# Deformable-convolution stage: waiting for the landing of the tile ahead in front of every second tile only

## The reference

```
offset  = conv2d(x, offset_w)                       # 18 maps: (dy, dx) for each of 9 taps
sy, sx  = base_y + dy, base_x + dx                  # where each tap of each pixel reads
y0, x0  = floor(sy), floor(sx);  ly, lx = sy - y0, sx - x0
p  = corner(y0,   x0,   (1-ly)*(1-lx)) + corner(y0,   x0+1, (1-ly)*lx)
p += corner(y0+1, x0,   ly*(1-lx))     + corner(y0+1, x0+1, ly*lx)   # gathered by index
y  = einsum('bckhw,ock->bohw', p, wk)               # [32, 64, 56, 56]
out = x + y * sigmoid(mean(y) + std(y))             # mean and std of each image and channel
```

## Time and profile before

| | |
|---|---|
| median of three runs | 15,070.81 us (15,065.17 to 15,072.31) |
| the profiled execution | 15,021.82 us |
| its span on the core | 15,020.2 us |
| mean granted clock of TensorE | 0.733 of full speed |
| busy: TensorE / weight load | 8857.2 us (59%) / 6070.3 us (40%) |
| busy: GpSimd / VectorE / ScalarE | 7518.3 us (50%) / 6520.5 us (43%) / 3085.6 us (21%) |
| first and last gather start | 3864.2 us and 14,983.5 us |

### The profile page before, as it was taken

One profiled execution on the slowest core, in us unless ns is written; L12 is line 12 of the kernel. 1 busy time (PEld: TensorE's weight loads), 2 busy tenths in 40 slices (PEclk: granted clock), 3 DMA queues, 4 the chain that ended last, 5 costly groups with the idle time before them and its releaser, 6 DMA issues.

```text
span 15020.2 us, 156851 instructions
## 1 busy us (share of the span) xinstructions
PE 8857.2 (59%) x51639; PEld 6070.3 (40%) x51639; DVE 6520.5 (43%) x13120; ACT 3085.6 (21%) x5214; POOL 7518.3 (50%) x7657
## 2 busy tenths in 40 slices
PE   6897888888554544545454545454454545454543
PEld 2333444448443433333343434343343434343433
DVE  5655556553334444343434343434434343434333
ACT  3433444432111111111111111111111111111111
POOL 0011222212466666666666666666666666666665
PEclk9998999989666666767676766666666657676766
DMA  3322111126333333333333333333333333333332
GB/s 95 84 82 66 52 60 56 56 99 189 96 91 109 91 108 99 101 99 101 106 96 103 98 109 91 109 91 109 99 102 102 98 103 96 104 98 109 91 94 83
DMA packets 503924, 1436.05 MB, mean 96 GB/s; under 512 B 128980, under 2 KB 234196, under 8 KB 474576
## 3 DMA queue, kind: packets, MB, share of 16 engines
q0 software_dynamic: 353344, 970.88, 22.2%
q1 hardware_dynamic: 150032, 458.00, 10.1%
HBM read 1175.46 MB, written 252.90 MB: 95 GB/s over the span
## 4 chain that ended last, share of the span: by engine, by line
POOL 29%; issue 19%; DMA 13%; DVE 8%; PE 6%; another core or an unknown queue 0%; DVEq 0%; POOLq 0%; ACT 0%; ACTq 0%; SPq 0%
POOL e_g L1786 29%; DMA e_g<-table_dram,e_index_slots 12%; DVE e_g L2050 2%; PE e_ps L1903 2%; DVE e_g L2052 2%; PE e_ps L1918 2%; PE e_ps L1930 2%; PE e_ps L1939 1%; DMA e_tmp<-x3s_dram 1%; DVE e_x3t L1963 1%; DVE e_index_slots L2024 1%; DVE e_x3t L1967 0%; DVE e_w_next L2008 0%; DVE e_st L1971 0%
## 5 line engine op out<-in xcount | busy, mean ns | idle before, releaser
L1786 POOL DMA_INDIRECT e_g<-table_dram,e_index_slots x7056 | 6823.6, 967 | 4426.0 <-issue 1893.4
L1930 PE MATMUL e_ps<-k_ident,e_g 128*128 128x128 f32 x7056 | 1719.1, 398 | 4897.7 <-DVE e_g L2052 4840.2
L1930 PEld LDWEIGHTS e_ps<-k_ident,e_g 128*128 128x128 f32 x7056 | 1153.8, 197 | 5455.4 <-DVE e_g L2052 5209.6
L1939 PE MATMUL e_ps<-e_corners,e_w_def 128*64 128x128 f32 x14112 | 2667.5, 369 | 268.6 <-issue 148.9
L2024 DVE COPY e_index_slots<-e_index_now 128x9 uint32<-128x9 uint32 (+1 forms) x784 | 137.9, 177 | 5866.8 <-DMA e_g<-table_dram,e_index_slots 4314.5
L1939 PEld LDWEIGHTS e_ps<-e_corners,e_w_def 128*64 128x64 f32 x14112 | 2430.1, 197 | 463.7 <-issue 319.0
L1855 ACT ACTIVATE e_corners<-e_ps 128x512 f32<-128x512 f32 (+1 forms) x2352 | 1064.7, 489 | 4603.2 <-PE e_ps L1930 3895.9
L2049 DVE TENSOR_TENSOR e_ps<-e_g,e_ps 128x512 f32<-128x512 f32 (+1 forms) x2352 | 1324.5, 563 | 115.6 <-DMA e_g<-table_dram,e_index_slots 61.1
L2052 DVE TENSOR_TENSOR e_g<-e_g,e_ps 128x512 f32<-128x512 f32 (+1 forms) x2352 | 1301.5, 553 | 81.3
L2050 DVE TENSOR_TENSOR e_g<-e_g,e_ps 128x512 f32<-128x512 f32 (+1 forms) x2352 | 1284.8, 546 | 0.0
L1860 ACT ACTIVATE e_big<-e_ps 64x128 f32<-64x128 f32 (+1 forms) x784 | 211.8, 270 | 3518.7 <-remote 2210.0
(11 more groups left out here) (438 smaller groups left out, 8075.1 us busy)
## 6 DMA issues: line engine op xcount, KB each, us to landing
e_g<-table_dram,e_index_slots POOLq DMA_INDIRECT x7056
table_dram<-e_rt SPq DMA_DIRECT2D x32, 1624.0 KB
a_xt<-x_in SPq DMA_DIRECT2D x16, 1568.0 KB
v_dram<-a_vout SPq DMA_DIRECT2D x32, 784.0 KB, 8.5
b_xt<-v_dram SPq DMA_DIRECT2D x16, 1568.0 KB
v_dram<-b_vout SPq DMA_DIRECT2D x32, 784.0 KB, 7.5
c_v2t<-v_dram SPq DMA_DIRECT2D x16, 1568.0 KB
c_xt<-x_in SPq DMA_DIRECT2D x16, 1568.0 KB, 6.6
```

Source lines behind the costliest of these rows:

```text
L1786: pool.indirect_dma_start(out=g[:, slot, tap * CORNERS:(tap + 1) * CORNERS], out_offset=None, in_=table, in_offset=bass.IndirectOffsetOnAx ...
L1930: mm = pe.transpose(ps[:, TURN[tap // 4], (tap % 4) * P:(tap % 4 + 1) * P], g[:, slot, tap * CORNERS:tap * CORNERS + 2 * C], k.ident[:, :])
L1939: mm = pe.matmul(ps[0:C, OUT, 0:P], w_d[:, tap, :], corners[:, tap, :], start=(tap == 0), stop=(tap == TAPS - 1))
```

## The change

GpSimd's wait for the landing of the tile ahead is kept in front of slots 2, 4 and 6 of the prologue and in front of slots 0, 2, 4 and 6 of every later round. In front of slots 1, 3 and 5 it is left out. The waits for the freed slot and for the indices stay everywhere, as do the order and number of the gathers. VectorE still waits for each slot's own landing.

```
                 for slot in range(SLOTS):
                     pool.wait_ge(index_ready, slot + 1)
-                    if slot:
+                    if slot and slot % 2 == 0:
                         pool.wait_ge(gathered[slot - 1], 16 * TAPS)
                     gather(slot)
                 with pool.Fori(1, PAIRS * GROUPS) as r:
                     for slot in range(SLOTS):
 
                         pool.wait_ge(bank_done, (r - 1) * (3 * SLOTS) + (3 * slot + 3))
-                        pool.wait_ge(gathered[(slot - 1) % SLOTS], r * (16 * TAPS) + (16 * TAPS if slot else 0))
+                        if slot % 2 == 0:
+                            pool.wait_ge(gathered[(slot - 1) % SLOTS], r * (16 * TAPS) + (16 * TAPS if slot else 0))
                         pause(pool, index_ready, r * SLOTS + (slot + 1), passed)
                         gather(slot)
```

## The result

The forecast was 14,110 us. The changed kernel takes **15,669 us** (median of four runs, 15,639 to 15,713) against 15,068 us of the kernel before: a ratio of 1.040, interval 1.037 to 1.043. It is 4% slower, and loaded a second time it took 15,843 us (1.053, 1.051 to 1.055). Both lie above the range and on the wrong side. The profiled execution took 15,712.6 us; its span is 690.7 us longer than that of before (15,710.9 against 15,020.2).

The account below looks back on a forecast made before the run. The prediction took GpSimd's chain of gather descriptors and landing waits to bound the deform stage. Dropped waits (810 us) plus stretched gaps (150 us) gave 960 us off 15,070.8, so 14,110 us, range 14,005 to 14,265.

Parts of the forecast that it names:

- What bounds the kernel now: Deform stage: GpSimd's chain of writing gather descriptors and waiting for landings, 13.6 us a tile, 10,700 us over 784 tiles.
- the false releaser at line 2024: VectorE's index copy, named by the page for 548 gaps; claimed to end together with the gap, both awaiting the same landing.
- the sequencer's cover: GpSimd's sequencer runs ahead; six queued gathers, some 7 us, hide the remaining waits, leaving 0.30 us at dropped waits.
- the first rival: Half the gap stays: uncovered sequencer work leaves 1.21 us at each dropped wait, 14,420 us; chance 0.08.
- The two terms of the sum: 336 dropped waits at 2.41 us give 810 us; stretched gaps beside bulk transfers give 150 us of 255.
- Nothing downstream is near its limit: Slots are freed early enough; per 697 us pair VectorE is busy 280 us and TensorE 350 us.
- The 50 us of the tightest refill: Smallest distance from VectorE's end of a tile to GpSimd's refill of its slot: 50.2 us of 777 refills, median 78.
- The waits that stay: In front of slots 0, 2, 4 and 6 GpSimd still waits 2.71 us, landing lag stays 1.8 us, cost 0.
- The sum: 810 + 150 = 960 us saved, taking 15,070.8 to 14,110 us, 6.4% faster.
- the gathers wait for something else: Rival: VectorE's index copy or the freed slot truly releases the gathers, so nothing changes, 15,070 us; chance 0.02.
- The slower rival: With up to 18 gathers under way the descriptor writer waits for room, each second-tile gather stretched 0.50 us, 15,780 us; chance 0.03.
- The signs named in the forecast: Expected profile: dropped gaps 0.30 us, gathers 946 ns, pair period near 637 us; freed-slot waits becoming real would mean wrong.

Follow-up runs that it names:

- e11: Changed kernel plus a waited-for one-column memset inside every tile, placed so no run of gathers exceeds six: 14,548 us, ratio 0.967.
- e10: Changed kernel plus a waited-for one-column memset after the fifth gather of every tile: 14,851 and, loaded again, 14,860 us, ratio 0.988 and 0.987.
- e7: Kernel before plus a waited-for one-column memset after the fifth gather of every tile: 15,777 us, ratio 1.051.
- e1: Changed kernel, its remaining landing waits kept, each gather also waiting for the landing of the third one before: 15,140 us, ratio 1.005.
- e2: Changed kernel without landing waits in front of any slot, each gather waiting for the landing of the third one before: 15,897 us, ratio 1.055.
- e6: Changed kernel with gathers of 512 bytes per pixel instead of 1 KB, part of the computation left out: 15,943 us, ratio 1.061.
- e3: Changed kernel plus a waited-for one-column memset in front of slots 1, 3 and 5: 14,672, 15,612 and 15,550 us in three loads.
- e5: Changed kernel without landing waits, a waited-for one-column memset in front of each slot but the first instead: 16,015 us, ratio 1.067.
- e4: Changed kernel with GpSimd's landing waits taken out for every slot, nothing in their place: 16,242 us, ratio 1.078.

## Why the prediction was wrong, step by step

*What bounds the kernel now*: right about GpSimd's chain and about the false releaser at line 2024. The dropped waits left 0.30, 0.43 and 0.38 us, as forecast, with the sequencer's cover as argued; the first rival (1.21 us) is refuted. The two terms of the sum, 810 + 150 = 960 us, measured 961 us together at the dropped waits.

*"Nothing downstream is near its limit"* is **the step that failed**. The 50 us of the tightest refill were read as slack of a chain whose own times stay. They did not stay: the delay from TensorE to ScalarE tripled with the length of GpSimd's runs, on the one pair of engines that every tile passes in order. In sum the 784 delays grew from 1418 to 4264 us, 25 us more in each round of seven tiles. The transposes' signals came late on top. That these delays and the shorter period that was wanted together used up the 50 us is argued from these sums; that the distance fell to 1.5 us and slot 0 waited in 90 of 111 rounds is counted. One entry of the page of before pointed there and was not followed: "remote" released 2210 us of ScalarE's idle time at line 1860, the largest entry there. Busy shares, which I used, do not show a late signal. And a range whose only uncertain terms were the landing lag and the excess had no term for what the runs of 18 do to others.

*The waits that stay* were put at a cost of 0, and here the whole loss stands: 1498 us in front of slot 0 and 178 us in front of slots 2, 4 and 6. The latter are 3.9, 3.5 and 3.2 us in the mean against 3.41, 2.84 and 2.72 before; the medians of slots 2 and 4 went to 4.2 and 4.0 us, and in the main the profile names "remote" as their releaser, not a landing.

*The sum* was right where the signals do come in time. For e11 it says 14,110 + 784 breaks: 498 us more of gaps within tiles were counted there (0.64 us a break), so 14,608 us; measured 14,548. For e10, 659 us of breaks, 14,769; measured 14,851 and 14,860. The excess of the gaps over 2.71 us, 264 us before by the same count, is 85 us in e11 and 221 us in e10: the 150 us forecast for it came in e11 (179) and not in e10 (43). That e11 hit the forecast rests on its one load.

*The rivals*: "the gathers wait for something else" had the right place, the freed slot, and was given 0.02 and no loss, since it was thought of as a bound already present and not as one that the change creates. The slower rival had the right sign by the wrong mechanism: its gathers of the second tile were to take longer, and they take 949 ns in the median as all others.

*The signs named in the forecast*: 0.30 us and 949 ns came as forecast, and "issue" rose by 467 times (336 forecast); the pair's period (743 us instead of 637) and "waits for the freed slot that become real" were the ones that tell of the error, though with TensorE and VectorE far from busy, not above 90%.

The Trainium skill's rule used for the forecast, on VectorE's two-input instructions beside GpSimd (SBUF — State Buffer, "Who interferes with whom"), changed nothing: the gathers' busy time fell by 38 us. The Trainium skill's page Perfetto Trace Analysis, "Tensor Engine Instruction (MATMUL, LD_WEIGHTS)", says that the profiler's end of a matmul is computed, and that the semaphore goes out only when PSUM has acknowledged the last write; this leaves room between a shown end and its signal, and the trace has up to 21.9 us there (31.5 in the second load).

**What stays open.** That pauses in GpSimd's descriptor writing shorten the delays is shown (e7, e10, e11), and that neither backlog nor bytes alone make them (e1, e2, e6). What holds the signals physically is not: whether the product or only its signal is late, why most of the late signals come while GpSimd is still writing, why breaks inside the tiles work and those at the edges fail in two loads of three (e3) and in e5, and what about a load picks the pattern.

## What to carry to other kernels

A slack measured on one side of a wait holds only as long as the services behind it keep their times; before removing a wait, ask what else the pause was good for, and look at the idle time that the profile gives to "remote". Where GpSimd writes gathers back to back beside TensorE, bound the runs: a pause of 0.8 us in every tile at runs of at most six gathers was worth more here, in one load, than the landing waits that it replaced; with breaks in every tile and runs of nine it was still 1.2% faster than before, in two loads. A gain of a few per cent from a ring of waits needs a second load before it is believed.

## What the runs showed of the hardware

- In the changed kernel TensorE's products reached ScalarE up to 21.9 us after their shown end while GpSimd wrote gathers back to back (31.5 us in its second load, 39.4 us in e4, 48.7 us in e2), while the writing itself did not slow (medians of 0.945 to 0.949 us for a gather in all kernels). ScalarE started 0.02 us behind the record of the raised semaphore.
- Pauses of 0.8 us more in the middle of each tile cut the mean delay from 1.8 to 0.5 us (e7).
- One and the same kernel took 14,672 and 15,612 us in two loads on one chip, while the medians of the kernel before stayed between 15,009 and 15,081 us in six sets of runs.
